# Sum of squares of the next layer's products from a Gram matrix of the transposed map; an output set issued as sixteen tiles

## The chip, the cores and the metric

One core of one Trainium2 chip runs the whole program. The metric is the device time of one execution in microseconds (us); lower is better. Three executions of the kernel before took 1352.03, 1356.14 and 1361.01 us, median 1356.14 us.

## The reference

A Fourier neural operator of four layers over 64 images of 64x64 pixels and 32 channels, in fp32, followed by a small attention and expert stage on the result. Of one layer:

```
x1 = _fourier_layer(v, W1, W2)            # rfft2, 12x12 modes kept twice, irfft2
x2 = jnp.einsum('bcxy,cd->bdxy', v, w_w[i]) + w_b[i][None, :, None, None]
v = x1 + x2
mean = jnp.mean(v, axis=(0, 2, 3), keepdims=True)
var = jnp.var(v, axis=(0, 2, 3), keepdims=True)
v = (v - mean) * jax.lax.rsqrt(var + BN_EPS)
v = v * bn_g[i][None, :, None, None] + bn_b[i][None, :, None, None]
if i < L - 1:
    v = jax.nn.relu(v)
```

The variance of x1 + x2 is found before either is computed for all pixels: the part of x1 and the cross part come from the modes, and the sum of squares of x2 is needed as a sum over all pixels of the squared products of the map with the next layer's weights. That last sum is what the change computes in another way.

## The kernel before, in words

A map of the 64 images is held as 16 quads of 4 images: 128 partitions (4 images x 32 channels) by 4096 pixels, worked on as two halves h of 2048 columns. There are three passes (l = 0, 1, 2); a pass runs over the quads and makes the normalized, clipped map of a layer and its spectrum. Between the passes lies the stage `mix(l)` (products of the modes, first inverse transform, variance, scale and shift), in which maps are not touched. After the third pass come a last mix and the token stage.

PSUM has eight banks of 512 columns. Banks 0 to 3 take map products, as two pairs; banks 4 to 7 take the spectra. For quad q of a pass TensorE does, in program order (line numbers of the profile in brackets):

- `out_set(l, q, h)`, once for each half: products of the old map with the layer's weights. In pass 0 they are made from features (L1646, four products of 32 rows by 512 columns); in passes 1 and 2 the first two quads are still on the chip (L1637) and the others are loaded, and go as 32x32 tiles (`blocks32`, L1621): eight products for banks 0 and 1, then, once the second pair of banks is free, eight for banks 2 and 3. On top comes the last inverse transform, 16 products ("turns", L1660). Each fp32 product stands in the trace as two weight loads and two matmul records.
- `y_transform(l, q - 1, yh)`, two times 16 products of 32x32 tiles (L1683), from `turned`, the transposed map.
- `next_set(l, q - 1, h)`: the finished map of quad q - 1 times the next layer's weights (L1621 again), into the same banks 0 to 3, only in order to be squared and summed.
- `x_transform(l, q - 1, b)`, two times 12 products with 128 rows and 64 columns of weights (L1695), from `spectra`.

The order on TensorE is out(q,0), y(q-1,0), next(q-1,0), y(q-1,1), out(q,1), x(q-1,0), next(q-1,1), x(q-1,1). ScalarE evacuates an output set with a fused scale, shift and relu (L1430), three of the four pairs; it squares and sums three of the four pairs of the next sets (L1439), and copies the modes (L1447). VectorE takes the fourth pair of each (L2036 and L2039; BN statistics, L2045), transposes the finished map (`turn_map`, L2061, twice a quad) and the y spectra (`turn_spectra`, L2074, twice a quad). `a_full` and `a_free` hand the pairs of banks back and forth; `set_of` numbers output sets and next sets in one sequence.

The SP queue stores each finished half (L1160 in passes 0 and 1, L1162 in pass 2), loads the half of quad q + 2 of the old map into the same slot that quad q left (L1165), and loads the half-inverted tiles (L1171). Two slots hold the old map and two the new one, so a load is issued once out(q, h) has been read, and is needed by out(q + 2, h). The placing of modes (L1109) and the weights of the modes (L1249) go by DMA, most from POOL. At the end of a pass the modes of the last two quads are placed by DMA, and only then `mix(l + 1)` starts on TensorE (L1548).

## Time and profile before

| | us |
|---|---|
| three runs, median (lowest to highest) | 1356.14 (1352.03 to 1361.01) |
| the profiled execution | 1348.81 |
| its span | 1347.0 |
| TensorE busy in the span | 1134.5 |
| VectorE busy | 855.6 |
| ScalarE busy | 551.6 |
| GpSimd busy | 367.7 |

The span is what the trace covers from its first instruction to its last. The profiled execution lies 7.33 us under the median of the runs. Busy time of TensorE is the time in which at least one matmul record is open; as up to sixteen tiles run at once, it is not a sum over matmuls. The granted clock is given as a share of full speed.

### The profile page before, as it was taken

The page shows a single profiled execution, that of the slowest core. Times are in us where ns is not written, and L with a number is a line of the kernel's source. Part 1 is how long each engine was busy: PE and PEld are TensorE (multiplying, and loading weights), DVE is VectorE, ACT ScalarE, POOL GpSimd, SP SyncE. Part 2 cuts the span into 40 slices and gives each one's busy share as a digit, 9 for nine tenths or more (in the row PEclk, how much of TensorE's full clock was granted, in tenths as well). Part 3 has the DMA queues.
Part 4 walks back from the last instruction along what each step waited for, and adds up shares of the span by engine and source line. Part 5 has one row for each costly group of instructions (what it writes and reads, how often), then busy time and mean ns, then how long its engine had stood idle before and what let it go on. Part 6 is the DMA issues. An engine that isn't in the chain of part 4 may idle for free.

```text
span 1347.0 us, 40550 instructions
## 1 busy us (share of the span) xinstructions
PE 1134.5 (84%) x18183; PEld 646.0 (48%) x18183; DVE 855.6 (64%) x1041; ACT 551.6 (41%) x808; POOL 367.7 (27%) x533
## 2 busy tenths in 40 slices
PE   4698899999969889899996989999899677954596
PEld 4444555555534445555554445555455352223552
DVE  6576676777747566666764856666666480058664
ACT  2165454444536444444443644444444380100150
POOL 8673113224235303121422630122222351100000
PEclk9899899999989999999997999999999898976789
DMA  6568999898328999999962789999997267931001
GB/s 165 139 192 221 274 248 226 211 232 200 101 89 202 233 318 351 337 361 330 363 203 59 198 219 342 351 336 370 327 355 230 43 269 257 379 110 42 1 0 32
DMA packets 156119, 300.29 MB, mean 223 GB/s; under 512 B 33064, under 2 KB 100024, under 8 KB 139012
## 3 DMA queue, kind: packets, MB, share of 16 engines
q1 hardware_dynamic: 131656, 251.53, 60.8%
q0 software_dynamic: 20864, 44.73, 11.5%
q8 instruction: 143, 2.34, 0.7%
q10 hardware_dynamic: 3426, 1.44, 0.4%
q14 instruction: 30, 0.25, 0.1%
HBM read 147.86 MB, written 128.48 MB: 205 GB/s over the span
## 4 chain that ended last, share of the span: by engine, by line
PE 56%; DMA 12%; DVE 11%; SPq 8%; ACT 6%; issue 5%; POOL 2%; DVEq 0%; ACTq 0%; POOLq 0%
PE ps L1621 14%; PE ps L1660 10%; PE ps L1695 7%; PE ps L1683 6%; PE ps L1584 4%; SPq L1160 3%; PE ps L1646 3%; PE ps L1548 3%; DMA half_inverse<-arena 2%; DMA arena<-maps 2%; SPq L1054 1%; PE ps L1563 1%; DMA maps<-arena 1%; PE ps L1523 1%; ACT arena L1430 1%
## 5 line engine op out<-in xcount | busy, mean ns | idle before, releaser
L1660 PEld LDWEIGHTS ps<-arena 48*128 48x128 f32 x3072 | 182.2, 190 | 86.3 <-issue 82.2
L1660 PE MATMUL ps<-arena 48*128 48x128 f32 x3072 | 201.4, 281 | 7.3 <-issue 3.2
L1430 ACT ACTIVATE arena<-ps,arena 128x1024 f32<-128x1024 f32 x96 | 112.3, 1202 | 221.5 <-PE ps L1660 203.4
L1109 POOL DMA_DIRECT2D arena<-arena x207 | 120.4, 589 | 301.9 <-ACT arena L1447 298.0
L1439 ACT ACTIVATE ps<-ps 128x1024 f32<-128x1024 f32 x144 | 145.5, 1011 | 98.7 <-PE ps L1621 98.4
L2074 DVE STREAM_TRANSPOSE arena<-ps 128x1024 f32<-128x1024 f32 x96 | 177.3, 1929 | 5.5 <-PE ps L1683 5.5
L1621 PE MATMUL ps<-arena 32*32 32x512 f32 x2944 | 160.3, 616 | 9.3 <-DMA arena<-maps 5.6
L1683 PE MATMUL ps<-arena 32*32 32x512 f32 x3072 | 152.2, 599 | 5.6 <-DVE arena L2061 3.4
L2061 DVE STREAM_TRANSPOSE arena<-arena 128x2048 f32<-128x2048 f32 x64 | 144.3, 2289 | 12.8 <-issue 6.4
L1695 PE MATMUL ps<-arena 128*64 128x96 f32 x2304 | 122.8, 257 | 32.7 <-DVE arena L2074 29.8
L1695 PEld LDWEIGHTS ps<-arena 128*64 128x64 f32 x2304 | 103.7, 142 | 87.6 <-issue 47.2
L1255 POOL TENSOR_SCALAR arena<-arena 32x384 f32<-32x384 f32 x96 | 112.4, 1171 | 83.4 <-DMA arena<-in_mode_w 77.1
L2036 DVE TENSOR_SCALAR arena<-ps,arena 128x1024 f32<-128x1024 f32 x32 | 43.0, 1343 | 117.5 <-PE ps L1660 117.5
L1621 PE MATMUL ps<-inputs,arena 32*32 32x512 f32 x1920 | 107.9, 613 | 7.7 <-issue 6.7
L1548 PE MATMUL ps<-arena 64*64 64x64 f32 x2304 | 79.9, 287 | 33.2 <-DMA arena<-arena 31.0
L1430 ACT ACTIVATE inputs<-ps,arena 128x1024 f32<-128x1024 f32 x48 | 56.1, 1202 | 120.7 <-PE ps L1660 120.7
L1548 PEld LDWEIGHTS ps<-arena 64*64 64x64 f32 x2304 | 65.3, 155 | 82.8 <-issue 71.6
L1249 POOL DMA_DIRECT2D arena<-in_mode_w x48 | 26.8, 566 | 260.0 <-ACT arena L1447 242.8
L2045 DVE BATCH_NORM_STATS2 arena<-ps 128x6 f32<-128x512 f32 x96 | 62.3, 690 | 40.9 <-PE ps L1621 40.9
L2061 DVE STREAM_TRANSPOSE arena<-inputs 128x2048 f32<-128x2048 f32 x32 | 72.5, 2308 | 8.1 <-ACT inputs L1430 4.0
L1621 PEld LDWEIGHTS ps<-arena 32*32 32x32 f32 x2944 | 39.7, 104 | 79.1 <-ACT arena L1430 30.0
L1035 ACT COPY arena<-ps 128x1024 f32<-128x1024 f32 x66 | 56.2, 857 | 50.2 <-PE ps L1584 50.2
(314 smaller groups left out, 1394.4 us busy)
## 6 DMA issues: line engine op xcount, KB each, us to landing
arena<-half_inverse SPq DMA_DIRECT2D x90, 384.0 KB, 12.1
half_inverse<-arena SPq DMA_DIRECT2D x120, 256.0 KB, 4.6
maps<-arena SPq DMA_DIRECT2D x112, 256.0 KB, 4.6
maps<-inputs SPq DMA_DIRECT2D x112, 256.0 KB, 12.4
arena<-maps SPq DMA_DIRECT2D x28, 1024.0 KB, 17.3
maps<-arena SPq DMA_DIRECT2D x28, 1024.0 KB, 18.0
inputs<-maps SPq DMA_DIRECT2D x28, 1024.0 KB, 21.7
arena<-in_mode_w POOLq DMA_DIRECT2D x48, 384.0 KB, 7.2
```

Of the source, the lines that this page charges most:

```text
L1109: eng.dma_start(dst, src).then_inc((modes_st[batch % 2], last_st, late_st)[part], 16)
L1255: nc.gpsimd.tensor_scalar(w, w, -1.0, None, ALU.mult).then_inc(signed, 1)
L1430: nc.scalar.activation(half(h_out(l, q), h)[:, 1024 * pair:1024 * pair + 1024], ps[:, 2 * pair:2 * pair + 2, :].rearrange("p b n -> p (b n ...
L1439: nc.scalar.activation(src, src, ACT.Square, accum_out=sums_x2[:, i:i + 1])\
L1548: last = nc.tensor.matmul(ps[64 * e:64 * e + 64, 2 * s + m, 0:384] .rearrange("p (b k) -> p k b", b=BATCH)[:, k], ring[2 * p + e][rows, 6 ...
L1621: last = nc.tensor.matmul(ps[32 * x:32 * x + 32, r, :], w[rows, 32 * r:32 * r + 32], source[rows, at:at + 512], start=True, stop=last_one)
L1660: last = nc.tensor.matmul(ps[:, b, at:at + 128], gtile[s][rows, 4 * b + 2 * h + n, :], iy[rows, :], start=False, stop=(i >= 2 and n == 1))
L1683: last = nc.tensor.matmul(ps[32 * x:32 * x + 32, 4 + r, :], fyt[rows, yh, :], src, start=(yh == 0), stop=(yh == 1))
L1695: last = nc.tensor.matmul(ps[64 * t:64 * t + 64, 4 + b, 96 * (y - 3 * b):96 * (y - 3 * b) + 96], spectra[:, at:at + 64], fx2[:, r, :], sta ...
L2045: last = nc.vector.bn_stats(stats[:, 12 * q + 6 * b:12 * q + 6 * b + 6], ps[:, 2 + b, :])
L2061: nc.vector.transpose(dst, src).then_inc(h_turned, 1)
L2074: nc.vector.transpose(dst, src).then_inc(y_turned, 1)
```

## The change

`next_set`, both `square` functions, the numbering of sets that went with them, and the sums over their results in `early_sums` are gone. In their place TensorE multiplies each chunk of 64 columns of the transposed map with itself: in `turned` a partition is a pixel and 64 columns are two images' or lines' channels, so that the product is a 64x64 Gram matrix of channels, accumulated in bank 6 on two column halves of the array (t = 0, 1). `gram_set` has 32 such products for each half, 64 for a quad. VectorE adds bank 6 to `gram` once a quad (`gram_add`, 128x64). At the start of the next mix `skip_energy` makes the wanted sum of the Gram matrix and the layer's weights: two products of 64x64, two VectorE products, two products with a column of ones, one copy.

The y spectra go to the banks in another order, so that bank 6 is emptied by the first of the two spectral transposes. `turn_map(q, h)` now waits until the Gram products of quad q - 1 have read its half of `turned`. The order on TensorE becomes out(q,0), y(q-1,0), y(q-1,1), out(q,1), gram(q-1,0), gram(q-1,1), x(q-1,0), x(q-1,1); in the drain after the last quad gram(15,1) comes behind x(15,1). `out_set` waits for both pairs of banks first and then issues all its products.

```diff
-            def square(l, q, h):
-                for pair in range(2 if h else 1):
-                    act.wait_ge(a_full[pair], set_of(l, "next", q, h) + 1)
-                    src = ps[:, 2 * pair:2 * pair + 2, :]
-                    i = 4 * q + 2 * h + pair
-                    nc.scalar.activation(src, src, ACT.Square, accum_out=sums_x2[:, i:i + 1])\
-                        .then_inc(a_free[pair], 1)
...
+            def banks_free(l, q, h):
+                if q or h:
+                    for pair in range(2):
+                        pe.wait_ge(a_free[pair], set_of(l, q, h))
+                else:
                     wait_group(pe, l, LAST_GROUPS + 3)
-                else:
                     pe.wait_ge(var_ready, l + 1)
-
-            def blocks32(w, source, h, pair, last_one):
-                for x in range(4):
-                    for r in (2 * pair, 2 * pair + 1):
-                        rows = slice(32 * r, 32 * r + 32)
-                        at = 2048 * h + 512 * x
-                        last = nc.tensor.matmul(ps[32 * x:32 * x + 32, r, :], w[rows, 32 * r:32 * r + 32],
-                                                source[rows, at:at + 512], start=True, stop=last_one)
-                return last
 
             def out_set(l, q, h):
                 s = q % 3
+                banks_free(l, q, h)
                 if l and q >= KEPT:
                     pe.wait_ge(ld[q % 2][h], loads(l, q // 2))
-                    for pair in range(2):
-                        free_pair(l, "out", q, h, pair)
-                        blocks32(wbd[l], h_in(l, q), h, pair, False)
+                    for x in range(4):
+                        at = 2048 * h + 512 * x
+                        for r in range(4):
+                            rows = slice(32 * r, 32 * r + 32)
+                            nc.tensor.matmul(ps[32 * x:32 * x + 32, r, :], wbd[l][rows, 32 * r:32 * r + 32],
+                                             h_in(l, q)[rows, at:at + 512], start=True, stop=False)
...
-            def next_set(l, q, h):
-                for pair in range(2):
-                    free_pair(l, "next", q, h, pair)
-                    blocks32(wbd[l + 1], h_out(l, q), h, pair, True).then_inc(a_full[pair], 1)
+            def gram_set(l, q, h):
+
+                n = quad_of(l, q)
+                pe.wait_ge(y_turned, 2 * n + 1)
+                for u in range(2):
+                    for k in range(16):
+                        t = k % 2
+                        pixels = turned[:, 2048 * u + 1024 * h + 64 * k:2048 * u + 1024 * h + 64 * k + 64]
+                        last = nc.tensor.matmul(ps[64 * t:64 * t + 64, 6, 0:64], pixels, pixels,
+                                                start=(h == 0 and u == 0 and k < 2), stop=(h == 1 and u == 1 and k >= 14))
+                last.then_inc(gram_full, 1)
+
+            def skip_energy(l):
+
+                pe.wait_ge(gram_ev, QUADS * l)
+                for t in range(2):
+                    rows = slice(64 * t, 64 * t + 64)
+                    last = nc.tensor.matmul(ps[rows, 7, 0:64], gram[rows], wbd[l][rows, rows], start=True, stop=True)
+                last.then_inc(skip_full, 1)
+                pe.wait_ge(skip_ready, 2 * l)
+                for t in range(2):
+                    rows = slice(64 * t, 64 * t + 64)
+                    last = nc.tensor.matmul(ps[rows, 7, 64:65], weighted[rows], ones[rows], start=True, stop=True)
+                last.then_inc(skip_full, 1)
 
...
                 if n:
                     pe.wait_ge(xs_ev, 2 * n)
                     pe.wait_ge(y_turned, 2 * n)
+                    pe.wait_ge(gram_ev, n)
...
-                        last = nc.tensor.matmul(ps[32 * x:32 * x + 32, 4 + r, :], fyt[rows, yh, :], src,
+                        last = nc.tensor.matmul(ps[32 * x:32 * x + 32, 6 - 2 * (r % 2) + r // 2, :], fyt[rows, yh, :], src,
                                                 start=(yh == 0), stop=(yh == 1))
...
                         y_transform(l, q - 1, 0)
-                        next_set(l, q - 1, 0)
                         y_transform(l, q - 1, 1)
                     if q < QUADS:
                         out_set(l, q, 1)
                     if q:
+                        gram_set(l, q - 1, 0)
+                        if q < QUADS:
+                            gram_set(l, q - 1, 1)
                         x_transform(l, q - 1, 0)
-                        next_set(l, q - 1, 1)
                         x_transform(l, q - 1, 1)
+                        if q == QUADS:
+                            gram_set(l, q - 1, 1)
...
-                if l:
-                    moments = stats.rearrange("p (n k) -> p k n", k=3)
-                    link(nc.vector.reduce_sum(f1, sums_x2, AX.X))
-                    link(stt(out=by_x, in0=moments[:, 1], scalar=256.0, in1=moments[:, 1], op0=ALU.mult, op1=ALU.mult))
-                    link(ttr(out=junk_x, in0=by_x, in1=moments[:, 2], scale=1.0, scalar=0.0, op0=ALU.add, op1=ALU.add,
-                             accum_out=f2))
-                    link(tt(x2_sum, f1, f2, ALU.add))
...
-            def square(l, q):
-
-                dve.wait_ge(a_full[1], set_of(l, "next", q, 0) + 1)
-                for b in range(2):
-                    last = nc.vector.bn_stats(stats[:, 12 * q + 6 * b:12 * q + 6 * b + 6], ps[:, 2 + b, :])
-                last.then_inc(a_free[1], 1)
+            def gram_add(l, q):
+
+                n = quad_of(l, q)
+                dve.wait_ge(gram_full, 2 * n + 2)
+                dve.wait_ge(gram_ev, n)
+                if q:
+                    tt(gram, ps[:, 6, 0:64], gram, ALU.add).then_inc(gram_ev, 1)
+                else:
+                    nc.vector.tensor_copy(gram, ps[:, 6, 0:64]).then_inc(gram_ev, 1)
+
+            def skip_energy(l):
+
+                dve.wait_ge(skip_full, 2 * l - 1)
+                for t in range(2):
+                    rows = slice(64 * t, 64 * t + 64)
+                    tt(weighted[rows], ps[rows, 7, 0:64], wbd[l][rows, rows], ALU.mult).then_inc(skip_ready, 1)
+                dve.wait_ge(skip_full, 2 * l)
+                link(nc.vector.tensor_copy(x2_sum, ps[:, 7, 64:65]))
+                dve.sem_inc(skip_read, 1)
...
-                    dve.wait_ge(y_full, n)
+                    dve.wait_ge(gram_full, 2 * n - 1 + h)
...
-                    src = ps[:, 4 + e:8:2, :].rearrange("p s (x c) -> p c x s", c=32)
+                    src = ps[:, 6 - 2 * e:8 - 2 * e, :].rearrange("p s (x c) -> p c x s", c=32)
...
-                        square(l, q - 1)
                         turn_spectra(l, q - 1)
                     if q < QUADS:
-                        for h in range(2):
-                            turn_map(l, q, h)
+                        turn_map(l, q, 0)
+                    if q:
+                        gram_add(l, q - 1)
+                    if q < QUADS:
+                        turn_map(l, q, 1)
```

## Rows read from the trace of the kernel before

**Rows 1.** Windows: busy time of each engine, granted clock, DMA share, GB/s, by pass.

```profile
157.20:358.80 201.60, 193.86 (x3330) 115.89 (x3328) 146.21 (x104) 95.55 (x143) 46.18 (x67) 1.00 0.85 216
484.50:685.80 201.30, 185.11 (x3666) 104.35 (x3650) 135.87 (x96) 88.41 (x132) 45.61 (x66) 0.98 1.03 342
825.80:1025.10 199.30, 185.21 (x3658) 104.29 (x3650) 136.37 (x96) 88.85 (x132) 45.55 (x66) 0.99 1.01 344
```

**Rows 2.** Timeline, PE, one quad of pass 0: start us, us, what [idle before].

```profile
218.43 2.06 PE L1660 MATMUL ps<-arena 48*128 48x128 f32 x32
220.42 1.14 PE L1683 MATMUL ps<-arena 32*32 32x512 f32 x32
221.43 1.24 PE L1621 MATMUL ps<-arena 32*32 32x512 f32 x24
...
222.60 1.62 PE L1683 MATMUL ps<-arena 32*32 32x512 f32 x30
224.15 1.53 PE L1646 MATMUL ps<-inputs,arena 32*128 32x512 f32 x8
225.61 2.06 PE L1660 MATMUL ps<-arena 48*128 48x128 f32 x32
228.15 1.21 PE L1695 MATMUL ps<-arena 128*64 128x96 f32 x24 [0.48 <-DVE arena L2074]
229.29 1.79 PE L1621 MATMUL ps<-arena 32*32 32x512 f32 x32
...
232.15 1.66 PE L1646 MATMUL ps<-inputs,arena 32*128 32x512 f32 x8
233.73 1.50 PE L1660 MATMUL ps<-arena 48*128 48x128 f32 x22
```

**Rows 3.** Timeline, PE, pass 1: an output set with both pairs free; a whole quad.

```profile
483.47 1.15 PE L1621 MATMUL ps<-arena 32*32 32x512 f32 x32 [1.57 <-DMA arena<-maps]
484.56 2.06 PE L1660 MATMUL ps<-arena 48*128 48x128 f32 x32
...
634.43 2.06 PE L1660 MATMUL ps<-arena 48*128 48x128 f32 x32
...
649.75 0.49 PE L1660 MATMUL ps<-arena 48*128 48x128 f32 x4
```

**Rows 4.** Timeline, short bursts: weight loads of 128 columns; products of 64 columns.

```profile
30.94 1.08 PEld L1511 LDWEIGHTS ps<-arena 128*128 128x128 f32 x9
1214.62 2.08 PE L520 MATMUL ps<-arena 64*64 64x64 f32 x64 [1.07 <-DVEq L741]
```

**Rows 5.** Line L1165, last first-half load of pass 1, then of pass 2.

```profile
L1165 SPq DMA_DIRECT2D arena<-maps x1: 6349/6349/6349, 673.9 to 673.9; - x1
DMA to landing us min/median/max: 20.9/20.9/20.9
...
L1165 SPq DMA_DIRECT2D inputs<-maps x1: 1280/1280/1280, 1013.7 to 1013.7; - x1
DMA to landing us min/median/max: 21.4/21.4/21.4
```

**Rows 6.** Timeline, PE: turns of quad 15 in pass 1, then in pass 2.

```profile
701.05 2.06 PE L1660 MATMUL ps<-arena 48*128 48x128 f32 x32
...
1042.55 0.72 PE L1660 MATMUL ps<-arena 48*128 48x128 f32 x8
```

**Rows 7.** Timeline, end of pass 0: PE, DVE and ACT.

```profile
373.39 1.15 PE L1683 MATMUL ps<-arena 32*32 32x512 f32 x32 [1.08 <-DVE arena L2061]
...
377.00 3.59 DVE L2074 STREAM_TRANSPOSE arena<-ps 128x1024 f32<-128x1024 f32 x2
380.64 2.19 PE L1695 MATMUL ps<-arena 128*64 128x96 f32 x24 [3.83 <-DVE arena L2074]
382.76 1.47 PE L1621 MATMUL ps<-arena 32*32 32x512 f32 x32
...
386.37 0.39 ACT L1447 COPY arena<-ps 128x288 f32<-128x288 f32 x1
...
392.65 1.59 PE L1548 MATMUL ps<-arena 64*64 64x64 f32 x48 [7.24 <-DMA arena<-arena]
```

73 lines of the change are left out of this document (29 added, 44 removed).

## Prediction

> **What bounds the kernel now.** I read the windows of the three passes first. In pass 0 TensorE is busy 193.86 of 201.60 us while the DMA engines are busy 0.85 of the time; in passes 1 and 2 it is busy 185 of some 200 us and the DMA share is 1.03 and 1.01, at 342 and 344 GB/s [rows 1]. The windows run over 13 quads in pass 0 and 12 in the others, so a quad takes 15.51, 16.78 and 16.61 us. Then the timeline of one quad: in pass 0 it is 218.43 to 233.73, 15.30 us, and TensorE has one gap, before L1695 [rows 2]. The undisturbed quad of pass 1 takes 15.32 us [rows 3], so passes 1 and 2 lose 1.46 and 1.29 us a quad to disturbance. The landings of loads say what lies beneath. The load of quad 15, first half, is issued at 673.9 and lands 20.9 us later, at 694.8, and in pass 2 at 1013.7 + 21.4 = 1035.1 [rows 5]; its turns start at 701.05 and 1042.55 [rows 6]. So pass 0 is bound by TensorE; passes 1 and 2 by TensorE and DMA nearly together, with 5 to 6 us of lead of the transfers at the end of a pass. DMA engines that are never idle can't deliver earlier because TensorE asks earlier.
>
> **What goes.** For each quad 32 products of 32x32 tiles (L1621), three squares on ScalarE, one pair of BN statistics on VectorE. ScalarE and VectorE have room in the passes (95.55 and 146.21 of 201.60 us [rows 1]), so their part counts for nothing in the steady state; it counts in the drain of a pass, below. On TensorE I read the pieces of a quad as distances between starts [rows 2]: turns 1.99; y 1.01; next set 1.17; second y 1.55; output products 1.46; turns and the gap 2.54; x 1.14; next set and second x 2.86, of which x is 1.14 and the next set 1.72; output products 1.58. Sum 15.30.
>
> **What comes.** 64 Gram products, 128 pairs of a weight load and a matmul record, with 64 columns of weights, 64 moving columns and two column halves of the array by turns. Two rows bracket the price. L1695 is the same layout with 96 moving columns: 24 records in 1.14 us to the next start, and 1.21 less the length of one, hence 42 ns each [rows 2]. L520 has 64 moving columns and 64 columns of weights on two tiles: 64 in 2.08 us, 29 to 32 ns each [rows 4]. If the moving columns set the pace, L1695 scaled by 64/96 gives 28. I take 29 ns, since two rows agree there, and 42 as the upper end; the lower end is 27. A quad then pays 128 x 0.029 = 3.7 us, and 0.13 for a change of block, as L1695 pays over its 24 x 0.042: 3.8 us (3.5 to 5.5).
>
> Here a rule of the notes speaks against the change. Nine loads of 128 columns take 1.08 us, of which the last 0.19 is one load's own length: 111 ns each [rows 4]. The Trainium skill (TensorE: Matmul & The Clock Gate, section LDWEIGHTS) puts a load at columns / 1.2 in ns, 107 for these, and the row agrees. By it a load of 64 columns is 53 ns; one after the other, 128 of them would be 6.8 us a quad and the kernel some 100 us slower. The row on L1695 denies that they go one after the other: its loads of 64 columns pass at 42 ns [rows 2].
>
> **The new quad in pass 0.** Turns 2 x 1.99, y 1.01 and 1.23, output products 2 x 1.46, x 2 x 1.14, Gram 3.82: 15.24 us. The second y loses the tail of the next set before it (I take 0.22 over the first, for the wider tiles that follow; between 0 and 0.54). The gap goes, because Gram and the second output set lie between the y products and x. The gain is 0.06 a quad, 0.8 us over 14. I count nothing for "sixteen at once" here: the output products are the four of L1646, already at 1.46 when both pairs are free.
>
> **Passes 1 and 2.** An output set whose pairs are both free takes 483.47 to 484.56, 1.09 us [rows 3], against 1.65 to 1.92 where the second pair is late. The new sets are always so, since the pair is no longer held by squares. New quad: 3.98 + 2.02 + 2.18 + 2.28 + 3.82 = 14.3 us, 1.0 less than 15.32. TensorE with the same disturbance would need 15.8 us. Over the 13 quads behind the first loads that is 13 us a pass, more than DMA lets through: the turns of quad 15 can start 1.09 us behind the landing, so the lead worth having is 701.05 - 694.8 - 1.09 = 5.2 us in pass 1 and 6.4 us in pass 2. I take 10.5 of the 11.5 (0 to 26).
>
> **Waits added.** `turn_map(q, 0)` waits for gram(q-1, 0): with the turns of out(q, 0) starting at T, y ends at T + 4, out(q, 1) at T + 7, the Gram halves at T + 9 and T + 11, and x at T + 13.2. Behind the waiting transposes of 2.3 us stand `gram_add` (128x64, a fraction of a us) and `turn_map(q, 1)`, which ends about T + 13.7; the y products of that quad want it at T + 16.3. 2.5 us of slack; not counted. Bank 6 is wanted by Gram at T + 7, and the first spectral transpose (1.8 us) ends at T + 6.2. The wait for both pairs before an output set costs nothing once no square holds them. No DMA is moved past another; the SP and POOL queues keep their order.
>
> **The drain of a pass.** From the start of the last y products to the last copy of modes: 373.39 to 386.76, 13.4 us; in it two spectral transposes of 3.59 us in which TensorE idles 3.83 us, x products at 2.12 us instead of 1.14, which is the lower of the two clock levels, and two squares ahead of the last copy [rows 7]. New: y 2.0, start of VectorE 0.3, first transpose 1.8, gram(15,0) 1.95 beside the second one, two x 2.3, copy 0.6: 9.0 us, 4.4 less. With the clock at its lower level through Gram and x it is 0.7 less. I take 3.5 for each pass, 10.5. The last quad before it is half hidden behind VectorE: 0.5 each, 1.5. gram(15,1) and `skip_energy` (some 2.0 and 1.5 us, 4 and 2 at the lower clock) have for cover the placing of modes, 386.76 to 392.65, 5.9 us [rows 7]; at the lower clock that cover is just used up. The four linked sums taken out of `early_sums` are weighed at nothing, up to 1 us a mix.
>
> **Sum.** 0.8 + 10.5 + 10.5 + 1.5 = 23.3 us, against the profiled 1348.81. That execution is 7.33 us below the median of runs; I take the gain off the median: 1356.1 - 23.3 = 1333 us.
>
> **Rivals.**
> A. DMA gives way: the transfers follow TensorE's new pace, and 13 us a pass come through instead of 5 and 6: 0.8 + 26.6 + 10.5 + 1.5 = 39.4, 1317 us. For it: some quads ran at 15.3 us in pass 1 [rows 3]. Against: a share of 1.01 to 1.03 over 12 quads. The Trainium skill (DMA: Bandwidth & Descriptors, section Bandwidth) gives 425 GB/s for one 16 MB transfer and 341 for 1 MB; by the first there is room above the 342 measured, by the second none. 0.13.
> B. The Gram products go at 42 ns, because two loads of 64 columns, and not the moving columns, set L1695's pace. Pass 0 then pays 128 x 0.013 = 1.7 us a quad, 23 over 14. Passes 1 and 2: 14.3 + 1.4 + 1.7 = 17.4 us a quad, 0.7 over the present 16.7, 26 quads, 19; the drains still give 8. Slower by 34: 1390 us. It decides from about 36 ns on, where pass 0 loses what the drains gain and the lead in passes 1 and 2 is not reached. For it: no row shows 128-row loads at less than 42. Against: L520 at 29 to 32. 0.12.
> C. The lead can't be cashed: TensorE now runs into every load, waits, is granted the lower clock after waits, and only the drains remain: 0.8 + 10.5 + 1.5 = 12.8, 1343 us. For it: a wait at the drain already brought the lower clock. 0.19.
> My forecast has 0.56.
>
> **Range and chances.** 1312 to 1352 holds the forecast with its bounds, A and C, and leaves B out. 1% (13.6 us) is what a measurement can tell from no change: faster 0.69 (forecast, A, a third of C), same 0.19, slower 0.12.
>
> **What would show it.** TensorE's matmul records rise by 3072 to 21,255. Right: the 128 Gram records of a quad start within 3.8 us; pass 0 stays at 15.2 to 15.3 us a quad; passes 1 and 2 fall to about 16.2 with DMA share 1.0, and output sets wait for loads; from last y to last copy 9 to 12 us. Wrong: quads of pass 0 above 16 us (B); quads of passes 1 and 2 below 16 (A); TensorE waiting for transposes L2061 (the slack of 2.5 us was not there).

## The result and the profile after

The change made the kernel slower: 1420.06 us, median of 4 runs (1410.83 to 1434.18), against 1357.01 for the kernel before (1352.03 to 1361.01, 4 runs). The ratio is 1.044, 95% interval 1.038 to 1.049. The forecast was 1333. The profiled execution of the change took 1434.18 us (span 1432.3), the longest of its four and 14 us above their median, and that of before 1348.81 (span 1347.0), 8 us below its own median, so that the two profiles lie 85 us apart where the medians lie 63 apart, and differences between these two profiles are upper ends.

First the windows of the three passes, from the turns of quad 2 on, over 13, 12 and 12 quads; they answer to [rows 1], with the same columns: window and its length, busy time of PE, PEld, DVE, ACT and POOL, granted clock, DMA share, GB/s.

```profile
159.50:368.80 209.30, 194.35 (x4164) 147.36 (x4160) 135.78 (x91) 55.99 (x65) 46.21 (x67) 0.97 0.85 207
493.30:732.20 238.90, 201.83 (x4431) 153.75 (x4416) 125.10 (x84) 51.77 (x60) 46.18 (x66) 0.89 0.97 293
873.30:1113.90 240.60, 199.86 (x4432) 148.23 (x4416) 126.38 (x84) 51.69 (x60) 46.66 (x66) 0.93 0.92 293
```

A quad takes 16.10, 19.91 and 20.05 us, where it took 15.51, 16.78 and 16.61. In passes 1 and 2 DMA moves 293 GB/s in place of 342 and 344, at shares of 0.97 and 0.92. That it is no longer what holds the passes is said by the waits for loads, below. TensorE's busy time does not fill the windows either (201.83 of 238.90), and its granted clock is 0.89 and 0.93 in place of 0.98 and 0.99. From the turns of quad 2 to those of quad 15 the passes lost 7.8, 38.3 and 38.2 us in the profiled executions. That is 84.2 of the 85.3 us between the spans. These are the windows of pass 1 over all 13 quads, first before, then the change:

```profile
484.56:701.05 216.49, 199.76 (x3961) 112.77 (x3952) 147.14 (x104) 95.75 (x143) 46.10 (x67) 0.98 1.00 333
493.34:748.08 254.74, 217.38 (x4793) 165.53 (x4784) 135.51 (x91) 56.08 (x65) 46.45 (x67) 0.90 0.93 283
```

Now TensorE's timeline in pass 0, which answers to [rows 2]: start, time, line, shape, records, idle time before. L1635 are the turns, L1679 y, L1621 the output products, L1647 Gram, L1691 x.

```profile
183.76 2.06 PE L1635 MATMUL ps<-arena 48*128 48x128 f32 x32
185.74 3.95 PE L1647 MATMUL ps<-arena 128*64 128x64 f32 x128
189.52 2.15 PE L1691 MATMUL ps<-arena 128*64 128x96 f32 x48
191.61 1.14 PE L1621 MATMUL ps<-inputs,arena 32*128 32x512 f32 x8
192.68 2.06 PE L1635 MATMUL ps<-arena 48*128 48x128 f32 x32
194.66 2.35 PE L1679 MATMUL ps<-arena 32*32 32x512 f32 x64
196.94 1.14 PE L1621 MATMUL ps<-inputs,arena 32*128 32x512 f32 x8
198.01 2.06 PE L1635 MATMUL ps<-arena 48*128 48x128 f32 x32
...
220.60 1.12 PE L1621 MATMUL ps<-inputs,arena 32*128 32x512 f32 x3
223.87 1.47 PE L1621 MATMUL ps<-inputs,arena 32*128 32x512 f32 x5 [2.14 <-issue]
225.27 3.79 PE L1635 MATMUL ps<-arena 48*128 48x128 f32 x32
228.99 3.29 PE L1679 MATMUL ps<-arena 32*32 32x512 f32 x64
232.21 1.14 PE L1621 MATMUL ps<-inputs,arena 32*128 32x512 f32 x8
```

The quad from 183.76 to 198.01 is undisturbed: 14.25 us, where before's was 15.30. Its 128 Gram records start within 3.78 us, 29.5 ns each. So the work of the change is 1.05 us a quad cheaper than what it replaces. Then, at 220.60, TensorE issues three of eight output products and stops. The next one starts at 223.87, and the releaser is "issue": no semaphore, no transfer of data. Behind the stop the turns take 3.79 us in place of 2.06.

The same in pass 1, with its clock:

```profile
560.75 4.12 PE L1647 MATMUL ps<-arena 128*64 128x64 f32 x127
...
564.77 1.34 PE L1691 MATMUL ps<-arena 128*64 128x96 f32 x28
571.03 1.86 PE L1691 MATMUL ps<-arena 128*64 128x96 f32 x19 [4.92 <-issue]
572.82 2.01 PE L1609 MATMUL ps<-arena 32*32 32x512 f32 x32
```

```profile
560.80:564.70 3.90, 3.90 (x129) 3.80 (x129) 2.48 (x2) 2.01 (x2) 1.44 (x3) 1.00 1.04 303
566.20:571.00 4.80, 0.00 (x0) 0.00 (x0) 1.64 (x1) 0.16 (x1) 0.00 (x0) 0.82 0.99 325
571.10:574.70 3.60, 3.60 (x51) 1.77 (x51) 0.00 (x0) 0.40 (x1) 0.00 (x0) 0.50 1.07 398
```

The three windows lie before, in and after the stop. The clock is 1.00 (2.4 GHz) before it, falls within it, and is 0.50, the lower level (1.2 GHz), after it; sixteen tiles (L1609) then take 1.94 us to the next start, in place of 1.09. What arrives during the stop is seen in the DMA queues. This is the line of the instruction queue in the window 568.5 to 569.6 us; in 566.0 to 568.5, the first half of the stop, that queue has no line.

```profile
q8 instruction: 1, 0.02, 5.7%
```

One packet of 16,384 bytes starts at 568.56 and takes 1.00 us: the stop is 2.7 us old when it starts, and ends 1.5 us after it has landed. The same holds in before and in every kernel below. In their passes there are 183 stops of more than 1.9 us that the profile puts down to "issue", and each ends 1.2 to 1.9 us after the landing of such a packet; at the 61 of 3 us or more the packet started only when TensorE had already stopped, 0.2 to 2.7 us before.

The number of packets says what they carry. The change has 168 in this queue, before 143; TensorE has 6,192 more records (matmuls and weight loads) for these 25 packets, 248 each. Over the 13 quads of pass 0 it is 33 against 26.

The waits of TensorE, whole pass 1 (turns of quad 2 to those of quad 15), say how much of this there is: line, whom it waited for, us in total, times, longest. First the kernel before (484 to 701 us), then the change (493 to 748).

```profile
PE ps L1695 <- DVE arena L2074: 5.8, 10, 0.8
PE ps L1621 <- DMA arena<-maps: 5.6, 3, 3.5
PE ps L1621 <- issue: 4.5, 5, 2.0
PE ps L1660 <- issue: 1.1, 1, 1.1
```

```profile
PE ps L1691 <- issue: 12.1, 4, 4.9
PE ps L1609 <- issue: 9.6, 3, 3.6
PE ps L1647 <- issue: 9.4, 7, 3.0
PE ps L1635 <- issue: 3.3, 2, 2.5
PE ps L1609 <- DMA arena<-maps: 2.2, 1, 2.2
```

With the small rest of the lines, "issue" goes from 6.4 to 35.1 us. In pass 2 it goes from 10.6 to 40.4. Loads, which the forecast took for the limit, account for 2.2. The median landing of half a map fell from 17.3 and 21.7 us to these:

```profile
arena<-maps SPq DMA_DIRECT2D x28, 1024.0 KB, 12.3
inputs<-maps SPq DMA_DIRECT2D x28, 1024.0 KB, 10.1
```

The drain of pass 0, which answers to [rows 7] (start, time, engine, line):

```profile
383.11 2.35 PE L1679 MATMUL ps<-arena 32*32 32x512 f32 x64 [0.99 <-DVE arena L2068]
...
385.50 3.69 DVE L2081 STREAM_TRANSPOSE arena<-ps 128x1024 f32<-128x1024 f32 x2 [2.44 <-PE ps L1679]
387.45 2.94 PE L1647 MATMUL ps<-arena 128*64 128x64 f32 x64 [1.99 <-DVE arena L2081]
390.17 2.94 PE L1691 MATMUL ps<-arena 128*64 128x96 f32 x48
...
393.16 0.40 ACT L1431 COPY arena<-ps 128x288 f32<-128x288 f32 x1 [0.59 <-PE ps L1691]
```

From the last y products to the end of the last copy it is 10.45 us, 2.9 less than before.

### The profile page after: what moved, and what is told of

It reads as the page before. It is cut to its first block, busy times and chain, and to the rows that moved or that the text cites. A ratio compares the mean times of both kernels' runs of the same rounds, so it can differ in the third digit from the quotient of the medians.

```text
span 1432.3 us, 46588 instructions
## 1 busy us (share of the span) xinstructions
PE 1181.9 (83%) x21279; PEld 810.3 (57%) x21279; DVE 814.4 (57%) x987; ACT 405.0 (28%) x520; POOL 368.4 (26%) x533
## 4 chain that ended last, share of the span: by engine, by line
PE 71%; issue 10%; DVE 9%; DMA 4%; ACT 3%; SPq 2%; POOL 1%; DVEq 0%; ACTq 0%; POOLq 0%
PE ps L1635 14%; PE ps L1647 13%; PE ps L1679 8%; PE ps L1691 7%; PE ps L1609 5%; PE ps L1566 4%; PE ps L1528 3%; PE ps L1621 3%; PE ps L1545 2%; PE ps L1614 2%; PE ps L1756 1%; PE ps L1503 1%; PE ps L626 1%; DVE ps L1912 1%; DMA arena<-arena 1%
## 5 line engine op out<-in xcount | busy, mean ns | idle before, releaser
L1635 PEld LDWEIGHTS ps<-arena 48*128 48x128 f32 x3072 | 198.0, 204 | 92.4 <-issue 92.4
L1647 PE MATMUL ps<-arena 128*64 128x64 f32 x6144 | 210.3, 232 | 40.8 <-issue 34.9
L1647 PEld LDWEIGHTS ps<-arena 128*64 128x64 f32 x6144 | 200.8, 146 | 52.0 <-issue 38.3
L1635 PE MATMUL ps<-arena 48*128 48x128 f32 x3072 | 218.2, 296 | 7.5 <-issue 5.7
L1101 POOL DMA_DIRECT2D arena<-arena x207 | 121.3, 594 | 335.8 <-ACT arena L1431 332.0
L2068 DVE STREAM_TRANSPOSE arena<-arena 128x2048 f32<-128x2048 f32 x64 | 147.5, 2305 | 72.2 <-PE ps L1647 63.0
L1679 PE MATMUL ps<-arena 32*32 32x512 f32 x3072 | 130.1, 635 | 11.7 <-issue 8.6
L1691 PE MATMUL ps<-arena 128*64 128x96 f32 x2304 | 113.5, 254 | 27.2 <-issue 27.1
L1691 PEld LDWEIGHTS ps<-arena 128*64 128x64 f32 x2304 | 104.9, 143 | 26.8 <-issue 26.7
L1431 ACT COPY arena<-ps 128x288 f32<-128x288 f32 x96 | 38.3, 399 | 278.9 <-PE ps L1691 278.9
L1679 PEld LDWEIGHTS ps<-arena 32*32 32x32 f32 x3072 | 41.8, 106 | 61.3 <-issue 48.2
L1057 POOL DMA_DIRECT2D arena<-arena x72 | 44.5, 625 | 62.7 <-DVE arena L1027 27.9
```

Source lines behind the costliest of these rows:

```text
L1101: eng.dma_start(dst, src).then_inc((modes_st[batch % 2], last_st, late_st)[part], 16)
L1635: last = nc.tensor.matmul(ps[:, b, at:at + 128], gtile[s][rows, 4 * b + 2 * h + n, :], iy[rows, :], start=False, stop=(i >= 2 and n == 1))
L1647: last = nc.tensor.matmul(ps[64 * t:64 * t + 64, 6, 0:64], pixels, pixels, start=(h == 0 and u == 0 and k < 2), stop=(h == 1 and u == 1 an ...
L1679: last = nc.tensor.matmul(ps[32 * x:32 * x + 32, 6 - 2 * (r % 2) + r // 2, :], fyt[rows, yh, :], src, start=(yh == 0), stop=(yh == 1))
L1691: last = nc.tensor.matmul(ps[64 * t:64 * t + 64, 4 + b, 96 * (y - 3 * b):96 * (y - 3 * b) + 96], spectra[:, at:at + 64], fx2[:, r, :], sta ...
L2068: nc.vector.transpose(dst, src).then_inc(h_turned, 1)
```

## The experiments

The theory after the profile: **late instructions**. The change gives TensorE 128 more records a quad (with the weight loads 736 in place of 608 in passes 1 and 2, 640 in place of 512 in pass 0) and 1 us less to issue them in: undisturbed, 52 records a us in place of 40 in passes 1 and 2, and 45 in place of 33 in pass 0. They come in transfers of 16,384 bytes through DMA engines that are full of map traffic. Where one is late TensorE stops for 2 to 5 us, and is often granted the lower clock after it. Rivals: the sixteen-at-once order; a fixed cost of the new waits; late map loads; Gram products that are dear in passes 1 and 2.

The table is read from the profiled execution of each kernel, from the turns of quad 2 to those of quad 15. A stop is more than 1.9 us between the starts of two TensorE records. Waits for loads count too; all in this table are in pass 1: four in half_gram, two in gram_bf16, one each in before, the change, gram_alone and gram_spread. The half-clock time is that at 0.50. Three numbers are passes 0, 1, 2.

| kernel | ratio to before (95%) | mean quad, us | stops | half clock, us |
|---|---|---|---|---|
| before | 1 | 15.5 / 16.7 / 16.7 | 0 / 2 / 1 | 0 / 7 / 3 |
| the change | 1.044 (1.038–1.049) | 16.1 / 19.6 / 19.6 | 5 / 10 / 13 | 14 / 51 / 34 |
| sixteen_alone | 1.012 (1.005–1.018) | 15.7 / 17.5 / 17.5 | 0 / 4 / 5 | 0 / 14 / 10 |
| gram_alone | 1.040 (1.031–1.048) | 16.2 / 19.0 / 19.3 | 4 / 12 / 13 | 14 / 38 / 34 |
| gram128 | 1.072 (1.065–1.080) | 17.9 / 19.3 / 18.3 | 0 / 2 / 0 | 0 / 10 / 0 |
| gram_wide | 1.056 (1.046–1.065) | 16.2 / 19.1 / 19.6 | 0 / 4 / 8 | 0 / 21 / 24 |
| gram_spread | 1.038 (1.030–1.045) | 16.1 / 19.0 / 19.1 | 5 / 13 / 12 | 10 / 27 / 27 |
| after_quiet | 0.988 (0.981–0.994) | 14.3 / 16.0 / 17.9 | 0 / 3 / 9 | 0 / 7 / 24 |
| before_quiet | 0.992 (0.989–0.996) | 15.3 / 15.8 / 17.5 | 0 / 1 / 8 | 0 / 0 / 14 |
| before_plain | 1.042 (1.035–1.050) | 15.3 / 19.2 / 19.2 | 0 / 0 / 0 | 0 / 0 / 0 |
| after_plain | 1.054 (1.048–1.060) | 15.2 / 19.6 / 20.2 | 3 / 1 / 2 | 0 / 0 / 7 |
| after_full | 1.066 (1.059–1.073) | 16.6 / 20.2 / 20.1 | 6 / 1 / 1 | 21 / 0 / 3 |
| half_gram | 0.962 (0.950–0.973) | 13.9 / 16.8 / 17.0 | 4 / 7 / 11 | 14 / 34 / 17 |
| gram_bf16 | 0.964 (0.956–0.972) | 12.6 / 16.8 / 16.8 | 1 / 12 / 10 | 3 / 27 / 34 |

### Which part of the change it is

**sixteen_alone**: the kernel before with the new order of an output set (both pairs of banks awaited first, then all products) and nothing else.

```diff
                     for pair in range(2):
                         free_pair(l, "out", q, h, pair)
-                        blocks32(wbd[l], h_in(l, q), h, pair, False)
+                    for x in range(4):
+                        at = 2048 * h + 512 * x
+                        for r in range(4):
...
```

> Only the issue of an output set is changed: the kernel before, with both pairs of banks awaited first and then all products of the set. Records per quad are those of before. The instruction-supply theory expects no loss: the ratio to before lies within 0.99 to 1.01, and stops of over 2 us stay as rare as before (three or four in all passes). A theory that the order of the tiles costs the time expects a good part of the 4.4% here. The prediction's own step (an output set in 1.09 us instead of 1.6 to 1.9) can't show, because squares still hold the second pair: below 0.5% either way.

Measured 1374.83 us (1369.23 to 1384.74), just above what was expected. The order costs 1.2% where the second pair is still held by squares: a quad of pass 0 goes from 15.30 to 15.40 undisturbed, passes 1 and 2 lose 0.8 us a quad (in an execution 10 us above the median). Here the theory missed: it expected stops as rare as before's, and "issue" in passes 1 and 2 went from 17 to 29 us with the number of records unchanged. The rest is waits for squares, 12.9 us in pass 1 (ScalarE's L1439 and VectorE's L2050).

**gram_alone**: the change with the 32x32 products of passes 1 and 2 pair by pair again; both pairs of banks are still awaited first.

```diff
-                    for x in range(4):
-                        at = 2048 * h + 512 * x
-                        for r in range(4):
+                    for pair in range(2):
+                        for x in range(4):
+                            at = 2048 * h + 512 * x
+                            for r in (2 * pair, 2 * pair + 1):
```

> The change without its sixteen-at-once order: the 32x32 products of an output set go pair of banks by pair of banks, as in the kernel before; everything else is the change. The order alone cost 1.2% on the kernel before. Late instructions: the order matters little and the Gram products are what costs, so 1390 to 1425 us, ratio to before 1.02 to 1.05. Rival (the two parts hinder each other, for instance because sixteen tiles in 1.09 us and the Gram burst together run the instruction buffer empty): 1350 to 1380 us.

Measured 1417.84 (1414.92 to 1423.38), beside 1361.95 for before. This is within the range. The intervals of 1.040 and of the change's 1.044 overlap. Most of the loss is in what this kernel keeps, the Gram products; what the order adds on top is too small to tell.

### Fewer records or longer records, with more work

**gram128**: Gram products of 128x128, of which two 64x64 blocks are used. 64 records a quad in place of 128, each four times the array.

```diff
-                    for k in range(16):
...
-                        last = nc.tensor.matmul(ps[64 * t:64 * t + 64, 6, 0:64], pixels, pixels,
+                    for k in range(8):
+                        pixels = turned[:, 2048 * u + 1024 * h + 128 * k:2048 * u + 1024 * h + 128 * k + 128]
+                        last = nc.tensor.matmul(ps[:, 6, 0:128], pixels, pixels,
```

> The changed kernel with Gram products of 128 columns by 128 columns: 32 instead of 64 a quad, so 128 records (loads and matmuls) fewer for each quad, the number of before, but on one tile at about 111 ns a record instead of 29.4: 7.1 us a quad instead of 3.8, 158 us more TensorE work in 48 quads. The instruction-supply theory expects stops of over 2 us to become rare and half clock with them, so that most of the 158 us is given back: 1400 to 1450 us. A theory in which the time is TensorE's own Gram work or the lower clock follows from dense work expects 1530 to 1580. A theory of late map transfers expects 1430 to 1500, with waits on loads gone.

Measured 1456.63 (1450.35 to 1464.55), 7 us above the range of the theory and far below the 1530 of the rival of TensorE's own work. The rival of late map transfers has 1430 to 1500, which holds it; against that one speak the waits, since in pass 1 of the change loads account for only 2.2 us, in gram128 for none, and the loads were left as they were. TensorE's undisturbed quad rose by 3.6 us, 173 over 48 quads; the time rose by 37. In passes 1 and 2 the quads are shorter than the change's (19.3 and 18.3 against 19.6), with two stops in place of 23. (Against gram_alone, 19.0 and 19.3, only those of pass 2 are.) This run changes two things at once, the number of records and their length. So the next one keeps the number.

**gram_wide**: 96 columns move in place of 64, the records and their order stay as they are.

```diff
-                        pixels = turned[:, 2048 * u + 1024 * h + 64 * k:2048 * u + 1024 * h + 64 * k + 64]
-                        last = nc.tensor.matmul(ps[64 * t:64 * t + 64, 6, 0:64], pixels, pixels,
+                        at = 2048 * u + 1024 * h + 64 * k
+                        pixels = turned[:, at:at + 64]
+                        last = nc.tensor.matmul(ps[64 * t:64 * t + 64, 6, 0:96], pixels,
+                                                turned[:, at - 32 * t:at - 32 * t + 96],
...
```

> The change with 96 columns moving in each Gram product in place of 64 (32 of them are not used): exactly as many records as the change, in the same order, with the same transfers, and only TensorE's time per Gram record longer. A tile with 96 moving columns takes 83 ns in the x transform, half of that where two column halves run side by side, so the record goes from 29.4 to about 42 ns and the undisturbed quad from 14.25 to about 15.9 us; 12.4 us x ... = 1.6 us x 48 quads = 77 us of added work. Late instructions (the theory): 736 records then fall into 15.9 us (46 a us in place of 52), stops of over 2 us become rare, and most of the 77 us is given back: 1400 to 1440 us, and the gap sums around the instruction transfers in passes 1 and 2 fall from 35 and 43 us to under 25. Rival (the order of the products or the semaphores costs a fixed time, whatever the rate): 1420 + 77 = 1497 us.

Measured 1442.97 (three of the four executions from 1429.35 to 1443.27, the fourth 1492.72; before 1361.95): 3 us above the range given, 54 below the rival's 1497. The timeline of pass 0 in this kernel, TensorE:

```profile
229.04 2.07 PE L1635 MATMUL ps<-arena 48*128 48x128 f32 x32
231.04 5.61 PE L1648 MATMUL ps<-arena 128*64 128x96 f32 x128
236.48 2.19 PE L1693 MATMUL ps<-arena 128*64 128x96 f32 x48
```

128 records in 5.44 us, 42.5 ns each, and the undisturbed quad is 16.10 us (at an upper clock that this one execution shows as 0.95). The work rose by 1.85 us a quad. The mean quad of pass 0 went from 16.10 to 16.22, and its five stops went to none: 1.7 of the 1.85 us were there before, as stops and slow clock. In passes 1 and 2 the quads are 19.1 and 19.6. Against the long profiled execution of the change (19.6 and 19.6) the whole 1.85 was free; against gram_alone and gram_spread (19.0 to 19.3) 1.3 to 1.7 of it was. Over the whole kernel 89 us of work were added and 23 us of time. This is the cleanest run of the set: as many instructions, the same transfers, only more time to issue them in. Its "issue" waits sum to 22.1 us in pass 1 and 22.7 in pass 2, in place of 35.1 and 40.4, as was expected (under 25). The largest of pass 1:

```profile
PE ps L1648 <- issue: 8.0, 5, 2.6
PE ps L1635 <- issue: 6.8, 5, 3.7
PE ps L1693 <- issue: 5.6, 2, 4.4
```

The places of the stops show what they hang on. TensorE's timeline of this kernel in pass 1:

```profile
572.81 1.35 PE L1693 MATMUL ps<-arena 128*64 128x96 f32 x28
578.59 1.87 PE L1693 MATMUL ps<-arena 128*64 128x96 f32 x19 [4.44 <-issue]
```

It is the stop behind the row at 564.77 in the change, behind the same 28 records of the x products, in another kernel and 8 us later. Both kernels have 21,279 matmul records, and this stop comes before number 8681 of them in both. Of the 12 stops of gram_wide 8 stand before the very record where the change stops too (for over 1.6 us), and so do 17 of the 28 of gram_alone that are put down to "issue". From one such stop of a pass to the next the distance is, in every kernel, within a few records of a multiple of 127 matmul records (381, 381, 634, 253 in the change's pass 1), and 127 with their 127 weight loads are what one transfer carries. So a stop lies where a block of instructions ends, and not at an event among the map transfers.

**gram_spread**: the first x transform between the two halves of Gram.

```diff
                         gram_set(l, q - 1, 0)
+                        x_transform(l, q - 1, 0)
                         if q < QUADS:
                             gram_set(l, q - 1, 1)
-                        x_transform(l, q - 1, 0)
                         x_transform(l, q - 1, 1)
```

> The change with the first x transform of a quad placed between its two halves of Gram products, so that the densest stretch (128 records at 29.4 ns) is half as long twice over. Late instructions by the average rate (736 records in 14.3 us): nothing gained, 1410 to 1440 us. Late instructions by the burst: stops fall, 1370 to 1400 us. The second VectorE turn starts about 1 us later and has over 5 us of room, so it should not show.

Measured 1415.74 (1407.72 to 1417.85, before 1361.95), in the range for the average rate and above that for the burst. It is not told apart from the change. With 30 stops against 28, taking the burst apart does not help.

### Less traffic

**after_quiet** and **before_quiet**: in either kernel a map store of passes 0 and 1 takes a quarter of its data, and so does an input load of every pass. The rest of each map is left out, so what later layers compute is not the reference's.

```diff
-                        sp.dma_start(blocks[j], src).then_inc(map_st[i % 2], 16)
+                        sp.dma_start(blocks[j][:, 0:1], src[:, 0:1]).then_inc(map_st[i % 2], 16)
...
-                sp.dma_start(half(h_in(l, i), h), maps_d[l - 1, ORDER[l][i], :, 2048 * h:2048 * h + 2048])\
+                sp.dma_start(half(h_in(l, i), h)[32 * 0:32], maps_d[l - 1, ORDER[l][i], 0:32, 2048 * h:2048 * h + 2048])\
```

> The changed kernel with little map traffic: in the first two passes only a quarter of each finished map is stored, and only 32 of 128 partitions are loaded back, so later layers work on stale rows. TensorE's instructions are unchanged. The instruction-supply theory (16 KB of instructions by DMA, late behind map traffic) expects the stops of 2 to 5 us and the half-clock stretches to nearly vanish, quads of 14.3 us in passes 0 and 1, total 1280 to 1320, faster than the quiet kernel before. A theory of late loads expects the same in passes 1 and 2 but no change in pass 0 (0.09 of its span lost as now). A theory in which denser matmul work itself lowers the clock expects the half-clock stretches to stay: 1390 or more.

> The kernel before with the same small map traffic (a quarter stored in the first two passes, 32 of 128 partitions loaded). Quads at TensorE's own 15.3 us in all passes: 1348.8 less 1.46 and 1.29 us on 13 quads each, about 1312, plus up to 20 us gained at the starts of the passes: 1295 to 1320. The instruction-supply theory expects it to be slower than the changed kernel under the same traffic by 20 to 50 us; a theory that the Gram products are worse in themselves expects it to be faster.

Measured 1343.45 for the change (2 runs, 1.1% below before) and 1348.96 for before (8 runs). Both totals missed their ranges (1280 to 1320 and 1295 to 1320), and the change is 5.5 us ahead, not the 20 to 50 expected. The windows of after_quiet, by pass, say why:

```profile
157.60:343.80 186.20, 185.84 (x4164) 142.11 (x4160) 135.53 (x91) 55.97 (x65) 46.25 (x67) 1.00 0.54 118
469.00:676.90 207.90, 194.74 (x4800) 149.78 (x4784) 135.51 (x92) 55.98 (x65) 46.43 (x67) 0.98 0.62 137
806.30:1038.70 232.40, 204.95 (x4800) 154.67 (x4784) 136.11 (x91) 56.08 (x65) 46.05 (x67) 0.95 0.76 204
```

In pass 0, at a DMA share of 0.54, TensorE is busy for 185.84 of 186.20 us and a quad takes 14.32 us in the mean, where the work needs 14.25: there the stops are gone, with instructions as many and as dense. In pass 1, at a share of 0.62, 13.1 us of "issue" remain, and in pass 2, whose stores were left whole, the change still stops nine times and before eight times. So less traffic took the stops of pass 0 away, but a share well below 1 does not keep them off. Nor does the amount of traffic order them: the kernel before stopped once in pass 2 with all its traffic (331 GB/s, 16.7 us a quad) and eight times with less (221 GB/s, 17.5 us a quad). Its quiet loads have another shape, 32 partitions in place of 128; which of the two did this no run separates.

What counts is the comparison of the two: quieting took 77 us off the change and 10 off before (1358.65 on that chip). Between the quiet kernels no difference is clear of noise (ratios 0.981 to 0.994 and 0.989 to 0.996). So the 4.4% are not in TensorE's work alone: with less traffic they are gone.

### Other work in passes 1 and 2

**after_plain** and **before_plain**: maps stored row by row in all passes, and four 128x128x512 products in place of the sixteen tiles. **after_full**: the change's stores, with those four products; it multiplies the regrouped map as if it were plain, so its maps of passes 1 and 2 are not the reference's. In the two plain kernels the stores are changed as well, of which the first lines show the condition:

```diff
-                if l < PASSES - 1:
+                if False:
...
-                    for x in range(4):
-                        at = 2048 * h + 512 * x
-                        for r in range(4):
-                            rows = slice(32 * r, 32 * r + 32)
-                            nc.tensor.matmul(ps[32 * x:32 * x + 32, r, :], wbd[l][rows, 32 * r:32 * r + 32],
-                                             h_in(l, q)[rows, at:at + 512], start=True, stop=False)
+                    for g in range(4):
+                        at = 2048 * h + 512 * g
+                        nc.tensor.matmul(ps[:, g, :], wbd[l], h_in(l, q)[:, at:at + 512], start=True, stop=False)
```

> The changed kernel with its maps stored as they lie (one transfer of 1 MB with 8 KB rows for each half in every pass, instead of four of 256 KB with 2 KB rows in passes 0 and 1), and so with output sets of four 128x128 products instead of sixteen 32x32 ones: 96 records a quad fewer in passes 1 and 2, 1.2 to 1.3 us more TensorE work there. The instruction-supply theory expects fewer records for each us and less load on the transfers that carry instructions: pass 0 at 14.3 us a quad, passes 1 and 2 at 15.6 to 17, in all 1330 to 1390 us. Without that theory it is the change plus 35 us of TensorE work, 1440 or more.

> The kernel before with the same plain maps and 128x128 output products, still pair by pair with the next sets. TensorE was 15.3 us a quad, and the second pair of an output set still waits for squares; four products take some 1.75 us where the pair order took 1.65 to 1.92, so no TensorE time is added or only 0.2 us a quad. Fewer records and lighter stores take away a part of the 1.46 and 1.29 us a quad that passes 1 and 2 lose: 1335 to 1360 us. If transfers of maps were not what delays instructions, it stays at 1355 to 1365.

> The changed kernel with only the output products of passes 1 and 2 altered: four of 128x128 instead of sixteen of 32x32, the transfers as they were (the columns of later layers then come in another order, which leaves the amount of work as it is). 96 records a quad fewer in 28 quads, 1.3 us a quad more TensorE work, 36 us in all. The instruction-supply theory expects the stops and half-clock stretches of passes 1 and 2 to fall by more than that costs: 1380 to 1415 us, below the changed kernel's 1420. A theory of late map transfers expects no gain, 1420 to 1440; a theory of dense work lowering the clock expects 1440 to 1456.

Measured 1436.61, 1421.54 and 1451.88 us (before 1358.9). All three missed their ranges (1330 to 1390, 1335 to 1360 and 1380 to 1415). I had priced the four products far too low: they take 3.63 us (before_plain, TensorE's timeline):

```profile
626.42 3.70 PE L1633 MATMUL ps<-arena 128*128 128x512 f32 x8
```

So the two kernels with Gram products have 5.1 us a quad more of TensorE work, not 1.3, and before_plain has 3.9 (19.23 us undisturbed against 15.30). They still answer. after_full adds 5.1 us in each of 28 quads, 143 us, and the time rises by 32; the stops of passes 1 and 2 go from 23 to 2 and the half clock from 85 to 3 us. Pass 0, where nothing was edited, has six stops (the change five). The total of after_full lies in the 1440 to 1456 of the rival by which dense work lowers the clock; but the half clock nearly vanished in the passes edited, so the match of the number is chance. before_plain, with the fewest and longest records, has no stop at all in three passes, and its quads of passes 1 and 2 take what TensorE needs, at DMA shares of 0.89 and 0.88.

### Fewer records and less work

**half_gram**: eight of the sixteen products of each half, so that only half of the sum is formed and the variance is not the reference's.

```diff
-                    for k in range(16):
+                    for k in range(8):
```

> The changed kernel with half of the Gram products left out (32 a quad; the sum of squares is then of half of the pixels): 128 records a quad fewer, as many as before the change, and 1.9 us a quad less TensorE work: 12.4 us a quad in pass 0, 90 us in all. The instruction-supply theory expects more than 90 us back where stops vanish, in passes 1 and 2 down to the pace of the map transfers (some 16 us): 1290 to 1340 us. If passes 1 and 2 stay above 17 us a quad with stops of over 2 us, fewer records do not cure it, as 12.4 us a quad keeps the records for each us as high as before.

**gram_bf16**: the change with the Gram products on the upper halves of the pixels.

```diff
-                        pixels = turned[:, 2048 * u + 1024 * h + 64 * k:2048 * u + 1024 * h + 64 * k + 64]
+                        at = 2 * (2048 * u + 1024 * h + 64 * k)
+                        pixels = turned.bitcast(mybir.dt.bfloat16)[:, at + 1:at + 128:2]
...
-                link(nc.vector.tensor_copy(x2_sum, ps[:, 7, 64:65]))
+                link(ts(x2_sum, ps[:, 7, 64:65], 1.00566, None, ALU.mult))
```

> The change with the Gram products taken from the upper halves of the fp32 pixels, read in place as bf16 at a stride of two; the sum is multiplied by 1.00566 for what cutting off the lower halves takes away on average. One record in place of two per product: 608 records a quad, as before the change, and 0.9 to 1.9 us of Gram products in place of 3.8. Undisturbed quad 11.4 to 12.3 us, which is 50 to 53 records a us, as dense as the change. Late instructions: stops and half-clock stretches stay at the change's size, total 1260 to 1320 us (half the Gram products at the same number of records came to 1310). Rival (stops come from the length of the Gram burst, which is halved): 1220 to 1250 us. Rival (a bf16 load at stride two runs slowly, over 60 ns a record): over 1330 us.

half_gram took 1310.13 us (2 runs), 110 below the change, of which 89 are the work left out (1.86 us in 48 quads): as many records as before's, but in 12.39 us. That is within the range. Of its 22 stops four, in pass 1, are waits for loads; the other 18 are fewer than the change's 27 that are put down to "issue", with 144 instruction transfers in place of 168. So fewer records at the same rate took a part of the stops away, most of it in pass 1. gram_bf16 took 1313.67 (1306.22 to 1320.65, 4 runs, before 1361.95), as the theory expected. It computes what the reference asks, with the sum of squares from bf16 operands and a constant for their mean loss, and beats both kernels: by 3.6% the one before. One product is one record instead of two, 64 in about 1 us (TensorE, pass 0, then its windows by pass):

```profile
214.87 1.22 PE L1648 MATMUL ps<-arena 128*64 128x64 bf16 x64
```

```profile
155.33:318.64 163.31, 155.88 (x3332) 108.62 (x3328) 135.68 (x92) 55.92 (x65) 46.32 (x67) 0.99 0.94 269
441.95:659.95 218.00, 175.02 (x3962) 119.27 (x3953) 134.42 (x91) 55.93 (x65) 46.00 (x67) 0.94 0.99 330
785.63:1003.42 217.79, 177.07 (x3963) 125.31 (x3953) 134.51 (x91) 56.15 (x65) 45.99 (x67) 0.92 0.97 323
```

Pass 0 falls to 12.6 us a quad, 38 us under before's. Passes 1 and 2 come to 16.8, as in before: TensorE needs some 11.5 us (11.55 undisturbed in pass 0), but it stops about as often as in the change, and the share of DMA is back at 0.99 and 0.97, with 7.8 us of waits for loads in pass 1. What these two passes could still gain from TensorE alone was not tried.

## Why the prediction was wrong

- **What bounds passes 1 and 2.** Right for the kernel before, and no use for the kernel after. DMA's pace was a floor for the quad, and I reasoned only about how near to the floor the quad would come. It went up to 19.6 us over 13 quads, away from the floor.
- **The failed step**: "TensorE with the same disturbance would need 15.8 us." I took the 1.46 and 1.29 us a quad that TensorE lost in passes 1 and 2 for a constant that goes with the traffic. They were in part stops for instructions (6.4 and 10.6 us of "issue" in passes 1 and 2), and those depend on how fast TensorE uses instructions up. Over 13 quads the time above the undisturbed quad was 2.7, 17.3 and 17.5 us by pass (201.58 - 13 x 15.30, 216.49 - 13 x 15.32, 216.68 - 13 x 15.32). After the change it is 24.1, 69.5 and 69.6 (209.36, 254.74 and 254.83, less 13 x 14.25). The difference is 126 us; the shorter quad gives back 42; 84 is what the passes lost. gram_spread, profiled within 1 us of its median, has 61.4 and 63.2 us in passes 1 and 2, so some 7 us a pass of the change's figure belong to its long execution. gram_wide shows it from the other side: with 1.85 us more work a quad the disturbance falls by 1.7 in pass 0 and by 1.3 to 1.7 in passes 1 and 2 against gram_alone and gram_spread.
- **The price of a Gram record**: 29 ns predicted, 29.5 measured. The Trainium skill (TensorE: Matmul & The Clock Gate, section LDWEIGHTS) gives a load its columns / 1.2 in ns, 53 for 64 columns; that would be the price if the loads went one after the other, and where two column halves take turns they do not. Rival B, 42 ns a record, is out too.
- **The quad of pass 0**: 15.24 us predicted, 14.25 undisturbed. The mis-sized terms are the output products, 1.07 to the next start and not 1.46 each (in before the second pair waited for a square there; sixteen_alone, which waits first, has its products in 1.07 as well), which is 0.78 of the 0.99 us. The two x products took 2.09 for 2.28, the Gram block 3.78 for 3.82, the two y 2.28 for 2.24. An error in favour of the change; it made the record rate higher still.
- **Passes 1 and 2, undisturbed**: 14.3 predicted, 14.24 the shortest.
- **The slack of 2.5 us at `turn_map`**: enough. In the steady state no wait of TensorE for the transposes shows in pass 1, where before had 5.8 us of waits for L2074.
- **The drains**: 3.5 us each predicted, 10.45 us from last y to last copy in the range of 9 to 12 given, so 2.9 gained. From the turns of quad 15 to those of quad 2 of the next pass the sum is -1.3 and +0.5 us; the early quads of a pass give the drain's gain back.
- **Rival C** had the clock: "waits, is granted the lower clock after waits." It had the clock's part right and the wait wrong, loads where it was instructions, and it missed that the stops would be more and longer: its price was 1343 us. No rival comes near 1420; B, the slow one, ended at 1390 for a reason that is not there. **Rival A** was the reverse of what happened: DMA's share fell below 1.
- Records: 21,255 predicted and 21,279 in the trace. Two slips in the prediction's own arithmetic change nothing: 0.69 for faster is the forecast and A alone (with a third of C it is 0.75), and 0.7 us over 26 quads in B is 18, not 19.

What was in the trace of before and could have warned: "issue" among the waits of TensorE, up to 2 us each in passes 1 and 2, and a queue of instructions beside 342 GB/s of traffic. The number of records was in the prediction and never priced.

What stays open. That late instructions are the cause of the stops rests on four things: each of the 183 stops put down to "issue" ends 1.2 to 1.9 us behind the landing of a transfer of 16,384 bytes; the stops stand where a block of instructions ends, often before the same record in different kernels; they become fewer with more time for the same instructions (gram_wide); and in pass 0 they vanish with less traffic (after_quiet). Why a block comes late is less sure. That it is the map traffic is argued from pass 0 of after_quiet, and pass 2 of before_quiet speaks against the amount alone. The path of a block of instructions was not moved by itself.

Nor does the rate alone say where a stop comes. In pass 0, undisturbed, before has 33 records a us and no stop, gram_wide 40 and none, half_gram 41 and four, gram_bf16 44 and one, the change 45 and five. The share of the slow clock in the loss was not separated. By the profile, 85 us at half clock in passes 1 and 2 cost at most 43 us of the 104 that the disturbance grew by there. But those 43 follow from the stops and don't stand beside them.

## What to carry to other kernels

Count the records that a change adds, not only TensorE's time: an fp32 product costs two matmul records and two weight loads, and in this kernel, near the limit of DMA, they were paid for in stops for instruction transfers. Where "issue" stands among TensorE's waits beside a DMA share near 1, price a change that makes the stream denser as slower until a run says otherwise. Fewer, larger products (gram128, after_full) took the stops of passes 1 and 2 almost away but cost more array time than that gave back; the one-record type, where its precision is enough, was faster than both kernels. And a loss seen at one pace ("the same disturbance") is no constant at another.

## What the runs showed of the hardware

- TensorE stopped for up to 4.9 us without a semaphore to wait for, until a 16,384-byte instruction transfer had come; it went on 1.2 to 1.9 us after the landing, at all 183 such stops, in 13 of the 14 kernels (before_plain has none). In after_quiet this happened at a DMA share of only 0.62.
- Such a transfer is spent after about 127 matmul records with their weight loads, and the stops stand at these borders.
- After 19 of the change's 28 stops the granted clock was 0.50 in the next microseconds (571.10 to 574.70 in the one shown), after the others it stayed at 1.00. In passes 1 and 2 of the change it was 85 us in all.
- Sixteen fp32 tiles of 32x32x512 take 1.09 us; four 128x128x512 products that hold the same data take 3.63, 454 ns for each of eight records.
- Two column halves taking turns pass an fp32 record of 64 moving columns in 29.5 ns and one of 96 in 42.5. In bf16 at a stride of two, 64 records take 1.04 us, 16 ns each.
